# A written-out order for every attention group of a fused transformer layer

## What is computed

```
x = x + attention(layernorm(x))       # 16 heads of 8 channels, causal
x = x + expert_ffn(layernorm(x))      # 8 experts, the best 2 per token, 512 rows each
# attention, per head:
att = (q @ k.T + bias[bucket(i - j)]) / sqrt(8)      # q, k rotated by position
att = softmax(where(j <= i, att, -inf)); y = att @ v
```

## Time and profile before

| | |
|---|---|
| median of the timed runs | 434.16 us |
| span of the profiled execution | 442.8 us |
| groups 0 to 7, first T to last T | from 51.9 to 337.3 us |
| PE, DVE, POOL, ACT busy | 89, 70, 61, 51% |

### The profile page before, as it was taken

One profiled execution on the slowest core, in us unless ns is written; L12 is line 12 of the kernel. 1 busy time (PEld: TensorE's weight loads), 2 busy tenths in 40 slices (PEclk: granted clock), 3 DMA queues, 4 the chain that ended last, 5 costly groups with the idle time before them and its releaser, 6 DMA issues.

```text
span 442.8 us, 7300 instructions
## 1 busy us (share of the span) xinstructions
PE 392.2 (89%) x2494; PEld 181.4 (41%) x2494; DVE 311.3 (70%) x727; ACT 227.7 (51%) x508; POOL 270.3 (61%) x243
## 2 busy tenths in 40 slices
PE   8986797999999999999989989999788589789891
PEld 2432343444434434344434533443233355455541
DVE  4686688766786776777896699886358577555547
ACT  1550153786766766766758665567575213223220
POOL 7376066387857969567568556968850644746640
PEclk9898698999999999999999999999899969999996
DMA  9486583300812403962301500000820122222127
GB/s 243 98 262 160 83 173 56 61 2 21 203 31 44 68 1 58 290 175 57 56 1 37 74 3 0 9 15 18 261 88 1 50 72 62 71 76 73 36 99 221
DMA packets 31661, 37.76 MB, mean 85 GB/s; under 512 B 5829, under 2 KB 26117, under 8 KB 31301
## 3 DMA queue, kind: packets, MB, share of 16 engines
q1 hardware_dynamic: 25578, 30.19, 28.9%
q0 software_dynamic: 2240, 4.21, 3.1%
q10 hardware_dynamic: 3808, 2.92, 2.4%
HBM read 28.84 MB, written 12.75 MB: 94 GB/s over the span
## 4 chain that ended last, share of the span: by engine, by line
PE 67%; issue 13%; DVE 12%; ACT 2%; DMA 2%; POOL 2%; SPq 1%; DVEq 0%; ACTq 0%; POOLq 0%
PE ps_slot L1067 13%; PE ps_av L1188 13%; PE ps_st L1159 12%; DVE neg_max L1430 6%; PE ps_slot L1071 5%; PE ps_st L1258 3%; PE ps_st L1011 3%; PE ps_slot L1268 3%; PE ps_st L1167 2%; PE ps_st L1260 2%; PE ps_slot L1239 2%; PE ps_slot L1219 1%; PE ps_av L1260 1%; ACT probs L958 1%; DMA q_parts<-part_all 1%
## 5 line engine op out<-in xcount | busy, mean ns | idle before, releaser
L958 ACT ACTIVATE probs<-ps_st 128x512 f32<-128x512 f32 (+3 forms) x384 | 168.8, 494 | 106.3 <-PE ps_st L1159 104.1
L1430 DVE TENSOR_REDUCE neg_max<-ps_slot 128x1 f32<-128x640 f32 (+7 forms) x184 | 176.1, 989 | 57.1 <-PE ps_slot L1071 55.0
L767 POOL TENSOR_TENSOR probs<-probs,f_all 128x960 f32<-128x960 f32 (+2 forms) x65 | 123.8, 1904 | 10.3 <-ACT probs L958 5.4
L1067 PE MATMUL ps_slot<-k_stack,q_stack 128*128 128x512 bf16 (+3 forms) x384 | 102.5, 337 | 9.3 <-DVE neg_max L1430 4.9
L1159 PE MATMUL ps_st<-q_stack,k_stack 128*128 128x512 bf16 (+3 forms) x384 | 104.4, 331 | 2.8 <-ACT probs L958 1.7
L1188 PE MATMUL ps_av<-probs,v_all 128*9 128x512 f32 (+3 forms) x768 | 80.4, 492 | 1.9 <-POOL probs L767 1.6
L764 POOL TENSOR_SCALAR_AFFINE_SELECT probs<-probs 128x512 f32<-128x512 f32 x58 | 37.2, 641 | 70.3 <-ACT probs L958 70.1
L1071 PE MATMUL ps_slot<-b_all,flip_b 128*128 128x240 bf16 (+2 forms) x288 | 67.2, 258 | 0.0
L1159 PEld LDWEIGHTS ps_st<-q_stack,k_stack 128*128 128x128 bf16 x384 | 35.1, 98 | 74.4 <-ACT probs L958 52.8
L1067 PEld LDWEIGHTS ps_slot<-k_stack,q_stack 128*128 128x128 bf16 x384 | 36.1, 99 | 44.8 <-DVE neg_max L1430 13.5
L777 POOL DMA_INDIRECT slots<-token_rows,slot_no x32 | 34.7, 1086 | 27.6 <-DVEq L1643 19.6
(11 more groups left out here) (208 smaller groups left out, 418.7 us busy)
## 6 DMA issues: line engine op xcount, KB each, us to landing
q_stack<-q_parts SPq DMA_DIRECT2D x21, 192.0 KB
slots<-in_c_rows_dram SPq DMA_DIRECT2D x4, 528.0 KB, 10.9
parts<-in_c_rows_dram SPq DMA_DIRECT2D x4, 512.0 KB, 10.7
q_stack<-parts SPq DMA_DIRECT2D x4, 512.0 KB, 5.5
k_stack<-k_parts SPq DMA_DIRECT2D x14, 128.0 KB
probs<-slots SPq DMA_DIRECT2D x6, 264.0 KB
f_all<-g_vec ACTq DMA_DIRECT2D x1, 1536.0 KB, 9.6
q_parts<-part_all SPq DMA_DIRECT2D x16, 96.0 KB, 3.7
```

What stands on the lines that cost most here:

```text
L767: pool.tensor_tensor(pr, pr, f_of[:, n % (H // HG), :, fo:fo + hi - lo], ALU.mult).then_inc(near_done, 1)
L958: act.activation(probs[:, u % PBUF, g, c0:512], ps_st[:, ST_NO[what] % 3, c0:512], ACT.Exp, scale=SCALE).then_inc(exp_done, 1)
L1067: pe.matmul(ps_slot[:, slot, o + lo:o + hi], q_stack[:, buf, t // MT, g, t % MT * P:(t % MT + 1) * P], k_stack[:, buf, lo // CW, g, 0:hi - ...
L1430: dve.tensor_reduce(neg_max[:, t // MT, heads[0]:heads[-1] + 1, t % MT], src, AX.X, ALU.max, negate=True).then_inc(slot_used, 1)
```

## The change

The tables `AV_LAG`, `AV_AT`, `Y_AT`, `M_LATE`, `S_BEFORE` and `M_BEFORE` and the functions `transposed_items` and `score_items` go. In their place stands one string a line, which `attention_plan` reads letter by letter: each letter takes the next unit of its kind. (The lines don't break exactly where groups of Ts do.) `AA` is a pair of value units with nothing of PE between. The number of units of each kind and their order among themselves are as before.

```diff
+ORDER = [
+    "SSSSSSSSSMSSSSSTSSTTTTTTSSTSTTTSSTTTSASATTMSASSSTTSTSTSATTTSAMTSTTSTSTSTSTATTSSTTASTSTTSTATTYSTTATSTSTATTST",
+    "TTSTSTAAMTSTTSTSTTSTATYTTSTTTSTTATTSSTTASTTSTTSASTTTSAMTSTTSTTSASTTSTAATSTTSTTTSTATTYT",
+    "TSTSATSTTSTSTTSAAMTTSTSTTATTSTTSTTSTATSTTSTSATTSTSTATSTTSATSTSTTTMAATTTYTSTTSTTATSTSTTAAY",
+    "TSTSTTTSSAAMTSTTSTTSTTATTYTTSTTTSAMTSTTSTASTTSATTTSSAYTTSTTSTATSSTTTATSTSTTTASTTTTSTTAA",
+    "TTTSSTAMTTSTSTTSATSTTSTTASTTTYTTSTMASTSTSTSTAASTTSTTTSTTATSTTSTTAATSTTSTTTSATTSTSTTAATS",
+    "TTSSTTTSTSAATMSTSTTSATSTYTTSTTTTTMATSTTATTAYTSTTATSTTSTATTSTTSTATTSTTTTATTSTATTTS",
+    "TTSTTSATSTTTSAASTTTMAYTSTATTSTTSTTSTTSTTSTATSTSTATSTSTATMTYTTSTSTATSTTSTATTSTTSATTSTTSAS",
+    "TTSTTSATSTTTATMTATTYTATTTYTTTTATTAATTTYTATTTATTTTTTTATTTTTATTTATTT",
 ]
+def heads_of(u):
+    return [(g,) for g in range(HG)]
 def attention_plan():
+    scores = [("S", n, su) for n in range(NG) for su in range(len(SUNITS))]
+    maxima = [("M", n, h) for n in range(NG) for h in range(NM)]
+    turned = [("ST", n, u, b) for n in range(NG) for u in range(NU) for b in range(len(heads_of(u)))]
+    values = [("AV", n, u) for n in range(NG) for u in range(NU)]
+    ends = [("Y", n, qb) for n in range(NG) for qb in range(2)]
     out = list(PROLOGUE)
-    scores = score_items()
-    for i, items in enumerate(transposed_items()):
-        while scores and scores[0][0] <= i:
-            out.append(scores.pop(0)[1])
-        out += items
+    for letter in "".join(ORDER):
+        what = {"S": scores, "M": maxima, "T": turned, "A": values, "Y": ends}[letter].pop(0)
+        out.append(what)
+        if letter == "T":
+            n, u, b = what[1:]
+            for g in heads_of(u)[b]:
+                out += EXTRAS.get((NU * n + u, g), [])
+        elif letter == "A" and what[2] in (CH - 1, NU - 1):
+            out.append(("EVAC", what[1], int(what[2] == NU - 1)))
     return out + LAST
```

In the same letters, the old plan of each of groups 1 to 3, from behind the last T of the group before to its own last T, reads `ATTSTTSTTMTATSSTATSTSTATTTSTTTSTTAYSTTTMTASSTTTSATSSTTATSSTYTTSSTATSTTSTTATSTTSATTTATST`. The rest of the diff lets a T stand for the heads that `heads_of` names; with single heads each engine's code issues what it issued:

```diff
-                    pe.matmul(ps_st[:, i % 3, c0:512], k_stack[:, n % NBUF, kt // CH, g, kt % CH * P:(kt % CH + 1) * P],
-                              q_stack[:, n % NBUF, qb, g, c0:512],
-                              start=True, stop=True).then_inc(scores, 1)
+                    for j, g in enumerate(heads_of(u)[b]):
+                        mm = pe.matmul(ps_st[:, i % 3, j * w:(j + 1) * w],
+                                       k_stack[:, n % NBUF, kt // CH, g, kt % CH * P:(kt % CH + 1) * P],
+                                       q_stack[:, n % NBUF, qb, g, c0:512], start=True, stop=True)
+                    mm.then_inc(scores, 1)
...
-                    act.activation(probs[:, u % PBUF, g, c0:512], ps_st[:, ST_NO[what] % 3, c0:512], ACT.Exp,
+                    src = ps_st[:, ST_NO[what] % 3, 0:len(heads) * (CW - c0)]
+                    act.activation(probs[:, u % PBUF, heads[0]:heads[-1] + 1, c0:512],
+                                   src.rearrange("p (g c) -> p g c", g=len(heads)), ACT.Exp,
                                    scale=SCALE).then_inc(exp_done, 1)
```

More of the change, by code:

```diff
@@ L54 @@
     + [(t, (g,)) for t in (4, 5, 6, 7) for g in range(HG)]
-AV_LAG = 3
-AV_AT = [0, 3, 1, 0, 4, 4, 3, 2, 3, 4, 3, 2]
-Y_AT = (7, 4)
 M_AT = (6, 22)
-M_LATE = 1
-S_BEFORE = [
[8 rows of a table removed]
+ORDER = [
[6 more added lines that the diff above has]
+    "TTSTTSATSTTTSAASTTTMAYTSTATTSTTSTTSTTSTTSTATSTSTATSTSTATMTYTTSTSTATSTTSTATTSTTSATTSTTSAS",
+    "TTSTTSATSTTTATMTATTYTATTTYTTTTATTAATTTYTATTTATTTTTTTTATTTTTATTTATTT",
 ]
-M_BEFORE = [(0, 16), (21, 54), (71, 102), (119, 150), (167, 198), (214, 245), (262, 300), (310, 342)]
 DISPATCH_AT = [73, 75, 77, 79, 81, 83, 84, 85, 86, 87, 88, 89, 90, 91, 92, 93]
@@ L174 @@
     + choose(2) + [("C", 3), ("PR", 2)] + place(2) + [("RI", 2)]
[L177 to L200, removed]
@@ L203, in score_items @@
[L203 to L215, removed]
@@ L239, in scores_of @@
 def scores_of(n, u):
-    return ST_NO["ST", n, u, HG - 1] + 1
+    return ST_NO["ST", n, u, len(heads_of(u)) - 1] + 1
 def fill_of(n):
@@ L827, in _ @@
                 elif kind == "ST":
-                    n, u, g = what[1:]
-                    if g == HG - 1 and u in NEAR and not (n == NG - 1 and u in LAST_NEAR):
+                    n, u, b = what[1:]
+                    if b == len(heads_of(u)) - 1 and u in NEAR and not (n == NG - 1 and u in LAST_NEAR):
                         near_product(n, u)
@@ L948, in _ @@
                 elif what[0] == "ST":
-                    n, u, g = what[1:]
+                    n, u, b = what[1:]
                     c0 = first_col(*UNITS[u])
+                    heads = heads_of(u)[b]
                     unit = NU * n + u
-                    if g == 0 and unit >= PBUF:
+                    if b == 0 and unit >= PBUF:
                         act.wait_ge(av_done, unit - PBUF + 1)
-                    elif g == 0 and unit >= 2:
+                    elif b == 0 and unit >= 2:
                         act.wait_ge(rope_done, 8)
                     act.wait_ge(scores, ST_NO[what] + 1)
-                    act.activation(probs[:, u % PBUF, g, c0:512], ps_st[:, ST_NO[what] % 3, c0:512], ACT.Exp,
+                    src = ps_st[:, ST_NO[what] % 3, 0:len(heads) * (CW - c0)]
+                    act.activation(probs[:, u % PBUF, heads[0]:heads[-1] + 1, c0:512],
+                                   src.rearrange("p (g c) -> p g c", g=len(heads)), ACT.Exp,
                                    scale=SCALE).then_inc(exp_done, 1)
@@ L1151, in _ @@
                 elif kind == "ST":
-                    n, u, g = what[1:]
+                    n, u, b = what[1:]
                     qb, kt = UNITS[u]
                     c0 = first_col(qb, kt)
-                    i = ST_NO[what]
-                    if g == 0 and (qb, kt) in ((0, 0), (1, 0)):
+                    i, w = ST_NO[what], CW - c0
+                    if b == 0 and (qb, kt) in ((0, 0), (1, 0)):
                         pe.wait_ge(mrows_in[qb], 16 * MAX_PARTS * (n + 1))
                     pe.wait_ge(exp_done, i - 2)
-                    pe.matmul(ps_st[:, i % 3, c0:512], k_stack[:, n % NBUF, kt // CH, g, kt % CH * P:(kt % CH + 1) * P],
-                              q_stack[:, n % NBUF, qb, g, c0:512],
-                              start=True, stop=True).then_inc(scores, 1)
+                    for j, g in enumerate(heads_of(u)[b]):
[3 more added lines that the diff above has]
+                    mm.then_inc(scores, 1)
                 elif kind == "FLIP":
```

## The result

The changed kernel took 421.82 us (median of 4 runs, 419.81 to 422.32) against 434.27 us (4 runs, 433.0 to 435.3) for the kernel before on the same chip: a ratio of 0.970, 95% interval 0.967 to 0.974. The forecast was 423.0 us in a range of 417 to 432. Run again later, against 11 runs of before, the same kernel gained a little more: 420.95 against 436.44 us, ratio 0.964 (0.960 to 0.968).

What follows compares the result with a forecast made beforehand. TensorE, busy 89% of the span, was taken to bound, with 33 us an order could win back. Terms -2.7 - 2.0 - 3.0 - 4.0 - 1.0 + 1.5 = -11.2 us took 434.2 to 423.0 us, range 417 to 432.

Steps and rivals of the forecast that it cites:

- the likeliest case: Whole kernel: the forecast holds and the time falls to 418 to 428 us; chance 0.60.
- Pairs, -2.7: TensorE's value units: 13 more back-to-back pairs each save 0.21 us of going in and out, 2.7 us.
- the 1.4 that was worked out from the Trainium skill: Value unit pairs on TensorE: estimate from array drains at tiling mode changes, 13 x 0.11 = 1.4 us saved.
- Output turns and maxima of groups 1 to 3, -2.0: Groups 1 to 3: waits at first output turns and behind maxima go; 3.2 us, of which 2.0 taken.
- a count of score units closer than 2.0 us: Score units beginning under 2.0 us behind the second before: 78 old, 81 new, 44 us short both times.
- Groups 4 to 6, -3.0: Groups 4 to 6: fewer score units beside DVE's router steps, fewer reduction waits; 3.0 of 10.0 us lost comes back.
- the marker of under 2 us in 190 to 289: Before the last group: PE's waits for reductions total under 2 us, where 200 to 306 had 3.6.
- Group 7, -4.0, to 29.0 us: Group 7: shorter T-run shortages, POOL waits and clock loss win back 4.0 of 9.3 us, despite 1.9 moved in.
- Start and group 0, -1.0: Start and group 0: maxima waits shrink, but DVE is slower from 38 to 75 us, so only 1.0 us saved.
- New waits for near products, +1.5: Value units with fewer T's ahead wait for POOL's near product: four late ones at 0.4 us, +1.5 us.
- Spans: From group 7's last T to the end: length stays 105.5 us; the saving is taken over to the timed median.
- One sign of being wrong: PE's score units: waiting for DVE as long as before would show the forecast wrong.

Runs made afterwards that it cites:

- no_pairs: The changed kernel with its 13 new pairs split, the second value unit one transposed product later; 423.29 us, ratio 0.970 to the kernel before.
- no_near5: The changed kernel with GpSimd's masks and near products of group 5 left out but for one column each; 414.93 us, ratio 0.952 to the kernel before.
- after: The changed kernel itself, with the whole new order against the kernel before, in its first run and trace; 421.82 us, ratio 0.970.
- after, again: The changed kernel, unedited, timed and traced a second time; 420.95 us, ratio 0.964 to the kernel before.
- first_half: The new order in groups 0 to 3, the old order from group 4 on; 428.35 us, ratio 0.982 to the kernel before.
- early_values: The changed kernel with every value unit three transposed products earlier, pairs kept; 470.2 us, ratio 1.079 to the kernel before.
- x_later: The changed kernel with ScalarE's step before group 7's last exponentials tied to a later value unit; 421.91 us, ratio 0.966 to the kernel before.
- router2: The changed kernel with router choice steps moved in group 5 and three placing steps tied behind POOL's products; 421.26 us, ratio 0.965 to the kernel before.

## Why the prediction was right

The forecast of 423.0 lies 1.2 us from the first result and 2 from the second, and the likeliest case was the one that came. The terms, one by one.

- **Pairs, -2.7.** Shown: no_pairs costs 2.3 to 2.7 us, near the rows' 0.21 a pair and above the 1.4 that was worked out from the Trainium skill.
- **Output turns and maxima of groups 1 to 3, -2.0.** Mis-sized. The 0.55 us ahead of the first Y is gone and the groups take 6.7 us less. Of that some 1.3 are the six pairs and an estimated 1 is value units that now stand elsewhere, so over 4 us are waits. None of PE's idle time is left. The full 3.2 of the sum would have been nearer: it was cut to 2.0 after a count of score units closer than 2.0 us, which said that short waits would come back. None did.
- **Groups 4 to 6, -3.0.** The stretch gained 6.9 to 7.3 us, but 1.3 of it are the six pairs and an estimated 2 to 3 is work, above all score units, that moved to group 7. What is left, some 3 us, is the size that was forecast, and its reason was wrong. The step that failed is that DVE "runs router steps between them, two of them 1.35 and 1.77 us long". They are 0.2 us long and held by POOL's product (no_near5). Having fewer score units in that stretch did not shorten the waits: the marker of under 2 us in 190 to 289 came out at 4.6 in four waits, each behind a held step. Without POOL's products in group 5, three of the four are gone, groups 5 and 6 together are 3.9 us shorter and the kernel 5 to 6 (not all of it need be the hold on DVE). PE's waits for reductions that are drawn as idle fell only from 5.3 to 4.6 here, so most of what was won is in waits under the pipelined tails, and no run shows which.
- **Group 7, -4.0, to 29.0 us.** Wrong in size and place. It takes 31.0 with the clock at 1.00. Some 1.5 of the four were put on the clock and two waits for POOL, but the clock drop belongs to one execution of before, not to its order: without it the old group 7 takes 29.8. The work moved in was also counted too low: four more score units, a value unit and an output turn are 3 to 3.5 us of PE's time by its usual pitches, not 1.9 (the prediction speaks of two score units). With that counted, the group's waits are some 4 us shorter than in the first trace of before, 1.9 of which go with the clock, and some 2 shorter than in the second. That work is missing in the groups before, so part of this term was booked under the wrong groups. One wait for POOL of 0.74 stays, at 301.24, and the last T waits 1.42.
- **Start and group 0, -1.0.** Mis-sized: group 0 is 3.8 to 4.9 us shorter in the traces. DVE, with 36.0 us of work in 47 now and 36.5 in 50 before, was not the bound there that the text made of it. PE's waits for DVE in the group fell from 3.3 to 1.6 us (the wait of 1.5 at the maxima is gone). The clock is a second part that the forecast left out: both traces of before have a stretch of it at the lower level, 70 to 74 us in the first (granted clock 0.60) and 72 to 76 in the second (0.61), where after and after, again show 1.00. How much of the gain is its, and what brought it back, is in no experiment by itself: open. The ratio of first_half (7.9 us for groups 0 to 3, of which groups 1 to 3 are 6.7 in the traces) speaks for the low end, or for an old group 0 that is usually shorter than in its two traces. Ahead of the first T nothing was won: the wait of 1.8 us at the first maxima went, but short waits of score units there grew from 0.5 to 2.4.
- **New waits for near products, +1.5.** None came: two waits of 1.1 us in all, where before had two of 1.6. early_values shows that the margin was less than three T's.
- **Spans.** The tail was said to stay at 105.5; it is 99 to 102 in every later trace, of either order. The first trace's 105.5 was that of one execution and no property of the order. Taking the saving over to the median of the timed runs, and not to the span, kept this out of the forecast.

Of the signs that were named, these came: no idle time ahead of the Y's, 13 more pairs, and a clock of 1.00 in group 7. These did not: under 2 us of waits before the last group, 29 us for group 7, no wait for POOL there, 105.5 us behind it. One sign of being wrong came: PE's score units wait for DVE longer than before, 8.1 us in 12 waits against 4.9 in 8, though the waits of score units, maxima and turns together fell from 11.6 to 8.1.

So groups 0 to 6 were forecast too small, group 7 too large, and the errors went against each other: -11.2 forecast, -12.4 to -15.5 measured. The direction and the pairs were understood; that the sum came as near as it did is in part luck.

## What to carry to other kernels

Where one engine bounds and its losses are waits of tenths, compare beginnings, group by group, after counting which work moved from group to group, and judge an order whole: half of a good one was slower than the old. A short step with one long instance is to be looked up on the other engines at the same moment before it is called long. And a wait that is removed ahead of a queue gives nothing until the wait behind it on the next queue is priced too; x_later and router2 each removed the wait they aimed at, for nothing. A clock drop seen in one trace is to be looked for in a second before it is booked as an order's cost.

## What the runs showed of the hardware

Some of DVE's small steps on SBUF stop while POOL runs its product of two SBUF tensors. Copies, tensor-scalar and two-input steps of 0.16 to 0.2 us took 0.83 to 2.21 us and ended within 0.1 us of its end, eight times in the rows of before, after and router2 above. Not every step is held. In after, a step with one input in PSUM (254.40, 0.21 us) and a reduction of an SBUF tensor (254.90, 0.22) ran at their usual length inside the product that began at 254.10. A reduction that reads PSUM shows nothing of it either: the one of 1024 columns at 257.97 in router2, all of it beside a product, took 1.22 us, and the two behind it (260.30), with no product beside them for nearly all their time, took 2.36 together.

It also works the other way, in after at 298 us:

```profile
297.76 1.35 DVE L1435 SCALAR_TENSOR_TENSOR probs<-probs,f_all 128x960 f32<-128x960 f32 x1 [1.09 <-ACT probs L926]
298.17 3.01 POOL L733 TENSOR_TENSOR probs<-probs,f_all 128x960 f32<-128x960 f32 x1
...
299.52 2.22 DVE L1435 SCALAR_TENSOR_TENSOR probs<-probs,f_all 128x512 f32<-128x512 f32 x1
```

POOL's product takes 3.01 instead of 2.23, as it began while DVE's of the same kind ran, and DVE's second takes 2.22 instead of the 0.69 of its like at 320.12. DVE's first ends at 299.11; 2.23 behind that is 301.34, near the 301.18 at which POOL's ends; DVE's second ends 0.56 behind that, at 301.74. So they ran one after the other. The Trainium skill (SBUF — State Buffer, Who interferes with whom) says that VectorE with two SBUF inputs contends with a GpSimd instruction that reads SBUF, and VectorE in a mode that uses both of its ports with GpSimd, that the first to issue holds the shared ports for its whole instruction, and that a reduction is free of it. The traces agree, with the rows above, for two-input steps, reductions and the order of issue; which mode the copies and tensor-scalar steps used they don't show. Had the forecast used that rule on the earlier trace rows, it would have asked where POOL's products fall, and not how many score units stand beside the router's steps.
